# The far unit's tail moved behind the next step's first fill in a fused attention block on one core

## What is computed

```python
h = layernorm(x) * (1 + ca) + sa
q, k, v = split(h @ W_attn)                       # 16 heads of 16
att = softmax(causal(q k^T / 4)) * decay           # decay: by distance, zero from 512 keys on
x = x + ga * ((att @ v) @ W_proj)
h = layernorm(x) * (1 + cb) + sb
x = x + gb * (h @ W^T + b + h @ (low-rank weight)^T)
```

## Time and profile before

| | us |
|---|---|
| median of 3 runs | 1539.15 (1534.87 to 1539.32) |
| profiled execution, its own time | 1538.15 |
| its span in the profile | 1535.4 |
| busy: PE, DVE, ACT, POOL | 1266.4, 1000.6, 1297.5, 203.1 |
| TensorE's granted clock, mean | 0.964 of 2.4 GHz |

### The profile page before, as it was taken

The page is one execution under the profiler, slowest core; times in us unless marked ns, Lnnn a source line. Parts: engine busy times, 40 slices in busy tenths (PEclk is TensorE's granted clock), DMA queues, the critical chain, the costliest instruction groups (busy, mean ns, idle before and its releaser), DMA issues.

```text
span 1535.4 us, 28806 instructions
## 1 busy us (share of the span) xinstructions
PE 1266.4 (82%) x11067; PEld 746.4 (49%) x11067; DVE 1000.6 (65%) x2058; ACT 1297.5 (85%) x2628; POOL 203.1 (13%) x429
## 2 busy tenths in 40 slices
PE   7875188898988898888888898989898888888774
PEld 5533044555555555555555555555555444444332
DVE  4642167777777777777777777777777666655552
ACT  3433089999999999999999999999999999999990
POOL 0322000020202011010202020202011110102022
PEclk9988589999999999999999999999999999999996
DMA  4999920000000000000000000000000000000000
GB/s 157 205 228 200 174 78 12 12 19 25 19 25 18 25 18 25 19 21 14 15 21 18 25 18 26 18 25 19 25 15 26 15 25 16 25 12 8 21 4 12
DMA packets 94448, 64.63 MB, mean 42 GB/s; under 512 B 59595, under 2 KB 89570, under 8 KB 94306
## 3 DMA queue, kind: packets, MB, share of 16 engines
q1 hardware_dynamic: 94306, 62.75, 18.0%
HBM read 41.74 MB, written 20.97 MB: 41 GB/s over the span
## 4 chain that ended last, share of the span: by engine, by line
PE 38%; DVE 26%; ACT 13%; issue 9%; POOL 1%; DMA 0%; SPq 0%; ACTq 0%; DVEq 0%
PE fast_s_ps L848 13%; DVE fast_negmax L1077 11%; PE fast_t_ps L897 10%; ACT fast_s_ps L1024 8%; DVE fast_probsT L1096 6%; PE fast_t_ps L866 5%; PE fast_t_ps L882 5%; ACT fast_probs L1024 5%; PE fast_t_ps L926 4%; DVE fast_probsT L1086 4%; DVE fast_y_sb L1115 1%; DVE fast_xb L1129 1%; DVE fast_xb L1152 1%; DVE fast_tT L1122 1%; PE fast_t_ps L908 1%
## 5 line engine op out<-in xcount | busy, mean ns | idle before, releaser
L1024 ACT ACTIVATE fast_s_ps<-fast_s_ps,fast_negmax 128x1024 f32<-128x1024 f32 (+4 forms) x768 | 786.1, 1025 | 12.3 <-PE fast_s_ps L848 11.6
L848 PE MATMUL fast_s_ps<-k_stack,fast_q_stack 96*128 96x512 bf16 (+3 forms) x2448 | 643.7, 354 | 123.4 <-ACT fast_probs L1024 83.3
L1024 ACT ACTIVATE fast_probs<-fast_s_ps,fast_negmax 128x640 f32<-128x640 f32 (+7 forms) x512 | 431.2, 842 | 66.2 <-DVE fast_negmax L1077 61.6
L1077 DVE TENSOR_REDUCE fast_negmax<-fast_s_ps 128x1 f32<-128x640 f32 (+4 forms) x512 | 397.8, 777 | 40.2 <-PE fast_s_ps L851 35.0
L1086 DVE TENSOR_TENSOR fast_probsT<-fast_t_ps,fast_dec_c 128x384 f32<-128x384 f32 (+2 forms) x512 | 276.5, 540 | 202.4 <-PE fast_t_ps L866 202.4
L848 PEld LDWEIGHTS fast_s_ps<-k_stack,fast_q_stack 96*128 96x128 bf16 x2448 | 203.1, 98 | 326.1 <-ACT fast_probs L1024 136.9
L866 PE MATMUL fast_t_ps<-ident,fast_probs 128*128 128x128 f32 x1488 | 252.4, 277 | 29.4 <-DVE fast_y_sb L1115 20.8
L1096 DVE TENSOR_TENSOR fast_probsT<-fast_t_ps,fast_dec_c 128x256 f32<-128x256 f32 x464 | 192.3, 414 | 115.0 <-PE fast_t_ps L882 115.0
L866 PEld LDWEIGHTS fast_t_ps<-ident,fast_probs 128*128 128x128 f32 x1488 | 172.3, 142 | 84.0 <-DVE fast_y_sb L1115 27.9
L882 PE MATMUL fast_t_ps<-ident,fast_probs 128*128 128x128 f32 x912 | 196.4, 296 | 20.1 <-DVE fast_tT L1122 6.4
L897 PE MATMUL fast_t_ps<-fast_probsT,fast_vals 128*16 128x128 f32 x4800 | 179.7, 275 | 23.3 <-DVE fast_probsT L1096 22.3
(11 more groups left out here) (110 smaller groups left out, 724.8 us busy)
## 6 DMA issues: line engine op xcount, KB each, us to landing
parts_d<-part SPq DMA_DIRECT2D x24, 512.0 KB, 11.5
k_stack<-parts_d SPq DMA_DIRECT2D x96, 128.0 KB, 7.4
fast_q_stack<-parts_d SPq DMA_DIRECT2D x384, 32.0 KB, 1.9
fast_vals<-v_d SPq DMA_DIRECT2D x36, 128.0 KB, 2.4
xs<-x_dram SPq DMA_DIRECT2D x8, 512.0 KB, 8.6
v_d<-w SPq DMA_DIRECT2D x8, 512.0 KB, 12.1
fast_xb<-x_dram SPq DMA_DIRECT2D x32, 128.0 KB, 2.2
out_dram<-fast_xb SPq DMA_DIRECT2D x32, 128.0 KB, 1.8
```

Source lines behind the costliest of these rows:

```text
L848: last = nc.tensor.matmul(s_ps[:, n % SLOTS, o:o + w], q, k_stack[:, h, P * b0 + o:P * b0 + o + w], start=True, stop=not diag)
L1024: nc.scalar.activation(dst, src, ACT.Exp, bias=negmax[:, p % 2, side, h:h + 1], scale=-1.0, accum_out=sums[:, p % 2, side, h, c:c + 1]).th ...
L1077: nc.vector.tensor_reduce(out=negmax[:, p % 2, side, h:h + 1], in_=s_ps[:, n % SLOTS, max(0, cols - P * WIN):cols], axis=AX_X, op=ALU.min) ...
```

## The change

In a step with value products, PE's `turn_tail(FAR, s)` and DVE's `decay_tail(FAR, s)` no longer stand at the end of step s. PE issues the two transposes behind `fill(s + 1, 0)`, DVE the multiplication behind `maximum(FAR, s + 1)`. The other steps keep their order. No number of a bank's user changes.

```diff
@@ PE, loop over the steps
                         fill(s, 0)
+                        if s > 0 and group_after(s - 1):
+                            turn_tail(FAR, s - 1)
                         if s > 0:
                             turn(NEAR, s - 1)
                             turn_tail(NEAR, s - 1)
@@
                         if group_after(s):
                             values(*group_after(s), 1)
                             fill(s, 4)
-                            turn_tail(FAR, s)
                         elif job_after(s, TAIL_JOBS):
@@ DVE, loop over the steps
                         maximum(FAR, s)
+                        if s > 0 and group_after(s - 1):
+                            decay_tail(FAR, s - 1)
                         if s > 0:
                             decay(NEAR, s - 1)
                             decay_tail(NEAR, s - 1)
@@
                             tail_job(*job_after(s, TAIL_JOBS))
-                        decay_tail(FAR, s)
+                        if not group_after(s):
+                            decay_tail(FAR, s)
```

## The result

| | before | changed |
|---|---|---|
| median of 5 runs, us | 1539.15 (1533.77 to 1540.07) | 1548.07 (1545.41 to 1552.09) |
| profiled execution, its own time | 1538.15 | 1550.13 |
| span | 1535.4 | 1547.5 |
| first far exponential of pair 0 | 196.65 | 200.04 |

The changed kernel is slower: the ratio is 1.0073, with a 95% interval of 1.0047 to 1.0099 (it is the ratio of the means; that of the medians is 1.0058). The two profiled executions differ by 12 us, more than the medians do. The last line says why: the first stage, whose code is the same, took 3.4 us longer in this one. What the change did is read from there on, and there the difference is 8.7 us.

What follows compares the result with a forecast made beforehand. The bound was taken to be a loop over DVE, ACT and PE in which each step hands on its delay. The terms summed to +10.5 us on the profiled 1538.15, so 1548.6; the median forecast was 1549, range 1541 to 1564.

Steps and rivals of the forecast that it cites:

- step 1: Step with reciprocals behind the near maximum, pairs 1 to 12: the 0.55 us delay goes through whole, +6.6 us.
- steps 11 and 13: Steps where DVE has only 0.33 and 0.31 us idle: about 0.15 us lost in each of 20, +3.0 us.
- plain steps: Steps 3, 5, 7, 9, 15 of pairs 1 to 3 and 8 to 11: 35 x 0.05 = +1.8 us.
- pair 4: Pair with a fifth fill of 1024 columns, which shortens the early start: 5 x 0.10 = +0.5 us.
- pairs 13 to 15: Last pairs, whose near tiles have no tail: only the gain, -2.0 us in all.
- The head start: Odd steps after value products: far fill and far maximum 0.49 us earlier, ACT's 0.33 us idle before the far exponential gone.
- The near tail 0.58 late: Same odd steps: near tail waits for DVE's later reading of the shared bank, starting at 300.44 instead of 299.86.
- PE's new wait: At the near tail's transposes, for DVE's multiplication of the far tail: some 0.3 us about 100 times.
- Rival A: Some 100 odd steps: near tail not held, far exponential 0.33 us earlier, -33 us to 1506; chance 0.05.
- Rival B: Slack in the loop absorbs half the reciprocal step's loss and the ordinary odd steps' cost: 1539 to 1543; chance 0.21.
- Rival C: Longer PE gap at each pair's reciprocal step lowers the clock in 12 pairs: +10 to +16 us, 1559 to 1565; chance 0.12.
- Rival D: Moved DVE multiplication loses both overlaps, near tail 0.17 us later still, 100 times: +17 us, 1566; chance 0.03.

Runs made afterwards that it cites:

- DVE's part alone: Against the kernel before, DVE's far multiplication moved behind the far maximum while PE kept its order: 1589.68 us, ratio 1.0334.
- the fastest version: Kernel before, far tail behind next far fill, near tail behind second fill, after value products; in pairs 13 to 15 after every step: 1503.14 us.

## Why the prediction was right

The prediction was 1549, slower, 1541 to 1564; 1548.07 was measured. The mechanism is the one that was forecast, and each term of the sum has its sign. With the two slow steps left out, the profiles have +6.8 us for step 1 (6.6 forecast), +3.7 for steps 11 and 13 (3.0), +2.5 for the plain steps (1.8), +0.6 for pair 4 (0.5), -1.1 for pairs 5, 6, 7 and 12 beside those (-0.6), +1.3 for pair 0 (1.2) and -2.5 for pairs 13 to 15 (-2.0). That the median came within 1 us of the forecast is partly luck: the runs of the kernel before alone scatter by some 6 us to either side.

- *The head start.* Right: the far maximum 0.48 to 0.49 early in pair 1, ACT's wait gone in the odd steps, 30 us less of it in all.
- *The near tail 0.58 late.* Right to 0.01 us, and it is the cause: with DVE's part alone the same 1.21 us between far maximum and near tail appear, and once PE has another fill to do in that time the kernel gains 1.8% in place of losing 0.7%, while that fill's new place alone gains nothing (1.0005).
- *PE's new wait* is there 102 times, but 0.70 us long, not the 0.3 that I had named. I had worked out when the near tail starts, not since when PE is idle: the far fill before it has moved forward too. The sum rests on the start and isn't touched. The near maximum starts 2.55 behind the far one, as forecast (2.56).
- *Step 1 of a pair, +6.6.* Right: 0.53 to 0.62 in each pair (steps 0 and 1 together), and it went away alone when step 0 was left out.
- *Plain steps, +0.05 each.* +0.07 each over the 35, coarse in detail. In pair 1 steps 3, 5, 7, 9 and 15 came out at +0.17, +0.04, -0.02, +0.07 and +0.08.
- *Steps 11 and 13, 0.15 each.* 0.23 and 0.13 in pair 1: the size was off by half for the one, the mechanism right.
- *Pair 4* was under-priced (1.76 against 1.3), pair 7 over-priced (0.03 against 0.4). Pairs 13 to 15 gained 2.5 rather than 2.0 us, without the step that the clock had lengthened; 1.6 of it is pair 15, where I had said about 1.
- *Rival A* (the head start goes through) fell with the bank still in the way, and is what the version with the near tail one fill later shows: -28 us where A had -33.
- *Rival B* (a wash): the interval of the ratio starts at 1.0047, so "no change" is outside it, and step 1 absorbed nothing.
- *Rival C* (the clock falls at step 1): its condition came true, its effect didn't. The gap at step 1 is 1.32 to 1.66 us long in pairs 1 to 12, yet between the stage's start (half clock up to about 205.8) and the work behind its last step (half clock from about 1519 on) the only stretch below full clock was in pair 14, at its step 13. In the kernel before, the clock had also fallen behind shorter gaps, at steps 1 and 13 of pair 14 (0.59 and 0.52 us). So the length of the gap alone doesn't decide it. Windows of the changed kernel (from:to and length, busy time of PE, PEld, DVE, ACT and POOL, granted clock, DMA share, GB/s), the first one with step 1 of pair 2, the second with step 13 of pair 14:

```profile
364.00:376.00 12.00, 9.52 (x102) 6.17 (x102) 8.22 (x19) 10.92 (x23) 0.00 (x0) 1.00 0.23 63
1416.00:1420.00 4.00, 3.48 (x13) 2.17 (x13) 1.42 (x4) 2.29 (x7) 0.00 (x0) 0.65 0.01 2
```

- *Rival D* (VectorE held between instructions): in the timeline above the moved multiplication starts 0.74 after a maximum that lasts 0.82, and its follower 0.33 after it though it lasts 0.41. It is so in all 126 places, so the overlaps are kept. The Trainium skill, "VectorE: DVE Perf Modes", section "The DRAIN you can't avoid", has the next operation wait until the pipe is empty, but adds that a next operation that is not held starts earlier. The prediction left this second half out, so its 0.57 us, and the 24 us worked out from it, are for a follower that is held. The followers here start before the recorded end of the instruction ahead of them, as the second half allows, and the prediction was wrong to say that the trace disagrees with the page.

## What to carry to other kernels

Where two users share one buffer in turn, moving the first one's reader later can move the second one's writer by as much (here 0.58 us), and with it everything that stands behind that writer in its engine's queue. Before you move a step for the sake of the engine that waits, walk the shared buffer's order through the other queues. And when such a move costs, ask first what could be issued ahead of the new wait: here one fill moved ahead of it turned +0.7% into -1.8%.

## What had not been expected

The same first stage ended at quite different times. The first far exponential in four profiled executions, whose code is the same up to there (before, changed, VectorE's part alone, move not made in step 0):

```profile
196.65 0.79 ACT L1024 ACTIVATE fast_probs<-fast_s_ps,fast_negmax 128x640 f32<-128x640 f32 x1 [12.84 <-DVE fast_negmax L1077]
```

```profile
200.04 0.79 ACT L1025 ACTIVATE fast_probs<-fast_s_ps,fast_negmax 128x640 f32<-128x640 f32 x1 [13.96 <-DVE fast_negmax L1078]
```

```profile
190.64 0.79 ACT L1024 ACTIVATE fast_probs<-fast_s_ps,fast_negmax 128x640 f32<-128x640 f32 x1 [12.69 <-DVE fast_negmax L1077]
```

```profile
200.59 0.80 ACT L1030 ACTIVATE fast_probs<-fast_s_ps,fast_negmax 128x640 f32<-128x640 f32 x1 [12.88 <-DVE fast_negmax L1083]
```

That is a spread of 10 us, and the runs of one kernel spread by 13 (1530.35 to 1543.06 for the kernel before), while steps whose order is the same repeat to about 0.02 us from one profile to the next where the clock does. Why the first stage varies wasn't looked into. So a difference of some us between two profiled executions says little here; the lengths of the pairs say it.

The other scatter is TensorE's clock. A step in which it falls is about 1.4 us longer, and the places wander: pairs 6 and 14 before, pair 14 after, pairs 6, 7 and 15 in the fastest version. The last stretch, behind the last step, where PE is busy a third of the time, ran at half clock in every version; here in the fastest (windows, columns as above):

```profile
1472.00:1480.00 8.00, 3.10 (x8) 1.49 (x7) 2.06 (x6) 0.00 (x0) 4.74 (x13) 0.50 0.00 0
1480.00:1488.00 8.00, 2.11 (x7) 1.53 (x8) 0.85 (x2) 0.00 (x0) 5.93 (x14) 0.50 0.00 0
```
